# Two graph-attention layers on one core: the last pair's second layer by batch, bias products in three pieces, new orders at both ends, and products of zeros first

## The reference

```python
# layer 0
q, k, v = x @ Wq + bq, x @ Wk + bk, x @ Wv + bv          # per head
attn = softmax(where(adj == 0, -inf, q @ k.T / sqrt(32)))
y = (attn @ v) @ Wo + bo + x
x = layernorm(y) * gamma + beta
# layer 1
q, k, v = x @ Wq.T + bq, x @ Wk.T + bk, x @ Wv.T + bv
pros = softmax(where(adj == 0, -16384, q @ k.T))
z = v
for _ in range(4):
    z = 0.9 * (pros @ z) + 0.1 * v                       # four hops
x = layernorm(x + z) * gamma + beta
```

## Time and profile before

| | us |
|---|---|
| median of three runs | 779.46 |
| runs | 778.97, 779.46, 779.46 |
| the profiled execution | 781.37 |
| its span, first to last instruction | 778.4 |
| TensorE busy in it | 751.4 |
| VectorE busy | 638.4 |
| ScalarE busy | 665.6 |
| GpSimd busy | 548.7 |

### The profile page before, as it was taken

The page is one execution under the profiler, slowest core; times in us unless marked ns, Lnnn a source line. Parts: engine busy times, 40 slices in busy tenths (PEclk is TensorE's granted clock), DMA queues, the critical chain, the costliest instruction groups (busy, mean ns, idle before and its releaser), DMA issues.

```text
span 778.4 us, 32533 instructions
## 1 busy us (share of the span) xinstructions
PE 751.4 (97%) x11544; PEld 708.3 (91%) x11544; DVE 638.4 (82%) x3093; ACT 665.6 (86%) x2570; POOL 548.7 (70%) x417
## 2 busy tenths in 40 slices
PE   6899999999999999999999999999999999999993
PEld 6788999999999999999999999999999999998973
DVE  5878888888888888888888888888888888888866
ACT  4879998889889888989988988998898998899771
POOL 0436858666777877777777777787777787768884
PEclk9999999999999999999999999999999999999998
DMA  7101011010111100111110111111011111000002
GB/s 240 49 21 51 23 35 37 21 31 23 51 49 51 50 27 26 51 51 49 51 39 27 35 51 50 49 51 30 22 51 50 50 50 37 21 11 30 30 15 68
DMA packets 33245, 34.12 MB, mean 44 GB/s; under 512 B 2368, under 2 KB 28864, under 8 KB 33088
## 3 DMA queue, kind: packets, MB, share of 16 engines
q1 hardware_dynamic: 33088, 32.06, 13.6%
HBM read 23.67 MB, written 8.39 MB: 41 GB/s over the span
## 4 chain that ended last, share of the span: by engine, by line
PE 89%; DVE 3%; ACT 2%; issue 1%; POOLq 0%; POOL 0%; DVEq 0%; ACTq 0%
PE psF L344 23%; PE psF L413 18%; PE psF L353 16%; PE psF L403 15%; PE psS L393 9%; PE psF L458 7%; PE psF L438 2%; ACT ex L1013 2%; DVE sm L1402 1%; DVE bst L1452 0%; DVE w_lo L1345 0%; ACT hT L1047 0%; DVE z L1515 0%; DVE hT L1418 0%; ACT pT L1024 0%
## 5 line engine op out<-in xcount | busy, mean ns | idle before, releaser
L1013 ACT ACTIVATE ex<-sm,nmax 128x128 f32<-128x128 f32 x1024 | 398.1, 397 | 3.3 <-DVE nmax L1402 2.3
L1862 POOL TENSOR_TENSOR pr<-ex,rec 128x1024 f32<-128x1024 f32 x128 | 245.4, 1919 | 99.2 <-DVE rec L1411 99.2
L1402 DVE CUSTOM_DVE_ANT_0 sm<-psS,mask 128x128 f32<-128x128 f32 x1024 | 228.3, 284 | 42.4 <-PE psS L393 42.2
L1013 ACT ACTIVATION_READ_ACCUMULATOR ex<-sm,nmax 128x1 f32 x1024 | 200.9, 196 | 0.0
L1024 ACT ACTIVATE pT<-psF 128x512 f32<-128x512 f32 x256 | 138.9, 597 | 34.4 <-PE psF L403 34.3
L403 PE MATMUL psF<-ident,pr 128*128 128x128 f32 x1024 | 137.8, 276 | 0.8 <-ACT pT L1024 0.5
L403 PEld LDWEIGHTS psF<-ident,pr 128*128 128x128 f32 x1024 | 112.7, 141 | 9.3 <-ACT pT L1024 0.9
L344 PE MATMUL psF<-xh,w_hi 128*128 128x256 f32 x512 | 112.2, 301 | 7.8 <-DVE w_lo L1341 5.8
L344 PE MATMUL psF<-xh,w_lo 128*128 128x256 f32 x512 | 103.9, 285 | 0.0
L344 PE MATMUL psF<-xl,w_hi 128*128 128x256 f32 x512 | 103.4, 284 | 0.0
L413 PE MATMUL psF<-pT,z 128*32 128x128 f32 x3072 | 101.5, 274 | 1.8 <-DVE z L1515 1.8
(11 more groups left out here) (76 smaller groups left out, 1426.2 us busy)
## 6 DMA issues: line engine op xcount, KB each, us to landing
xt_in<-in_x_t SPq DMA_DIRECT2D x32, 256.0 KB, 3.1
x_in<-in_x SPq DMA_DIRECT2D x32, 256.0 KB, 2.9
out<-o_t SPq DMA_DIRECT2D x30, 256.0 KB, 2.2
adj_in<-in_adj SPq DMA_DIRECT2D x32, 128.0 KB, 2.4
pT<-in_w SPq DMA_DIRECT2D x4, 256.0 KB, 4.4
row<-in_rows SPq DMA_DIRECT2D x1, 768.0 KB, 7.1
w_raw<-in_w SPq DMA_DIRECT2D x3, 256.0 KB, 7.6
out<-o_t SPq DMA_DIRECT2D x4, 128.0 KB, 1.8
```

What stands on the lines that cost most here:

```text
L1013: e = nc.scalar.activation(ex[l][:, b, h, :], sm[l][:, b, h, :], ACT.Exp, scale=-1.0, bias=nmax[l][:, b, h:h + 1], accum_out=tot[l][:, b, ...
L1402: last = nc.vector.tensor_tensor_reduce(sm[l][:, b, h, :], psS[:, o:o + N], mask[p.parity][:, b, :], -1.0, BIG, ALU.add, ALU.min, nmax[l][ ...
L1862: nc.gpsimd.tensor_tensor(pr[l][:, b, :, :], ex[l][:, b, :, :], rec[l][:, b, :].unsqueeze(2).broadcast_to([128, H, N]), ALU.mult).then_inc ...
```

## The change

1. **Zeros first.** VectorE sets a tile of 256 columns to zero as its first instruction; TensorE waits for it and multiplies it by itself five times, ahead of everything else.
2. **The folds in three pieces.** `folds()` becomes `fold_row` for weight 3 behind the scores of pair 0, `fold_row` for weight 6 between the two keys of pair 1, and `fold_columns` behind them. The saves on VectorE, the rounding and splitting of weights 3 to 6 are dealt out singly.
3. **Orders.** `begin()` now covers t up to 7, the loop runs from 8 to 29, and `end()` covers what was steps 30 and 31 too. In `begin()` and `end()` the order of each engine is dealt anew; `step(t)` is as before.
4. **The last pair's second layer by batch.** For pair 31, layer 1: reciprocals and probabilities for four heads at a time, (0, 0) and (1, 0) on GpSimd, (0, 1) and (1, 1) on VectorE; hops, copies, transposes and adds for one graph at a time, in the banks of the scores, which are free by then; all four copies of a graph on ScalarE; norm and output for one graph at a time.
5. `statistics` waits for the aggregate of the pair before.

```diff
+            nc.vector.memset(zeros[:, :], 0.0).then_inc(zeros_s, 1)
...
+            def keep_warm(times):
+                for _ in range(times):
+                    nc.tensor.matmul(ps_fold[:, :256], zeros[:, :128], zeros[:, :256], start=True, stop=True)
+            pe.wait_ge(zeros_s, 1)
+            keep_warm(WARM)                      # WARM = 5
...
             def begin():                         # TensorE
...
                 free((q_s[0], Pair(0)))
+                values(0, 1, Pair(0))
                 values(0, 0, Pair(0))
-                values(0, 1, Pair(0))
                 scores(0, Pair(0))
-                folds()
+                fold_row(0, 3, ps_fold_bo)
                 free((v_s[0], Pair(0)))
+                queries(0, 1, Pair(1))
                 queries(0, 0, Pair(1))
-                queries(0, 1, Pair(1))
                 free((k_s[0], Pair(0)))
                 keys(0, 0, Pair(1))
+                fold_row(1, 6, ps_fold)
                 keys(0, 1, Pair(1))
+                fold_columns()
...
             def begin():                         # VectorE
+                save_q(0, Pair(0))
                 make_mask(Pair(0))
-                save_q(0, Pair(0))
+                make_mask(Pair(1))
                 save_k(0, Pair(0))
+                split_lo(Pair(1))
                 mask_scores(0, 0, 1, Pair(0))
                 mask_scores(0, 1, 0, Pair(0))
-                split_lo(Pair(1))
                 mask_scores(0, 0, 0, Pair(0))
                 mask_scores(0, 1, 1, Pair(0))
+                save_q(0, Pair(1))
                 save_fold(0)
+                save_k(0, Pair(1))
+                reciprocals(0, 0, Pair(0))
+                split_w(3)
                 save_fold(1)
                 save_fold(2)
-                reciprocals(0, 0, Pair(0))
-                save_q(0, Pair(1))
-                save_k(0, Pair(1))
                 reciprocals(0, 1, Pair(0))
-                split_w(3)
-                make_mask(Pair(1))
...
             def begin():                         # ScalarE
+                round_w(3)
+                split_hi(Pair(1))
                 save_v(0, Pair(0))
-                split_hi(Pair(1))
...
-                for i in range(3, NW):
-                    round_w(i)
+                round_w(4)
                 split_hi(Pair(2))
...
                 save_oh(Pair(0))
+                round_w(5)
+                save_v(0, Pair(1))
...
                 save_x1h(Pair(0))
+                round_w(6)
                 split_hi(Pair(3))
...
             def begin():                         # GpSimd
-                add_bias(Pair(0))
                 probabilities(0, 0, Pair(0))
                 probabilities(0, 1, Pair(0))
+                add_bias(Pair(0))
...
+            def last_hop(j, b):
...
+                src = z[R.parity] if j else v1[R.parity]
+                for c in range(C):
+                    for g in range(G):
+                        h, o = G * c + g, 1024 * b + c * N
+                        last = nc.tensor.matmul(psS[32 * g:32 * g + 32, o:o + N], src[:, b, h * HD:(h + 1) * HD],
+                                                pT1[R.parity][:, b, h, :], start=True, stop=True)
+                last.then_inc(hop_r[b], 1)
+            def last_turn(j, b):
+                pe.wait_ge(hopT_s[b], j + 1)
+                for c in range(C):
+                    o = 1024 * b + 512 + c * 128
+                    last = nc.tensor.transpose(psS[:, o:o + 128], hT[R.parity][:, b * C + c, :], ident[:, :])
+                last.then_inc(turn_r[b], 1)
...
             def end():                           # TensorE, its last lines
                 turn_hop(3, Pair(29))
+                last_hop(0, 0)
+                last_hop(0, 1)
+                last_turn(0, 0)
+                last_turn(0, 1)
+                turn_hop(2, Pair(30))
+                last_hop(1, 0)
+                last_hop(1, 1)
+                hop(3, Pair(30))
+                last_turn(1, 0)
+                last_turn(1, 1)
+                turn_hop(3, Pair(30))
+                last_hop(2, 0)
+                last_hop(2, 1)
+                last_turn(2, 1)
+                last_turn(2, 0)
+                last_hop(3, 0)
+                last_hop(3, 1)
+                last_turn(3, 0)
+                last_turn(3, 1)
...
+            def last_evict(j, b):                # ScalarE
+                act.wait_ge(hop_r[b], j + 1)
...
+                nc.scalar.activation(hT[R.parity][:, b * C:(b + 1) * C, :],
+                                     psS[:, 1024 * b:1024 * b + D].rearrange("p (c n) -> p c n", n=N),
+                                     ACT.Copy, scale=1.0 - ALPHA).then_inc(hopT_s[b], 1)
...
             def end():                           # VectorE, its last lines
                 normalise(1, 0, Pair(28))
                 normalise(1, 1, Pair(28))
                 add_hop(3, Pair(29))
                 statistics(1, Pair(29))
+                last_add(0, 0)
                 aggregate(1, Pair(29))
+                last_add(0, 1)
                 add_hop(2, Pair(30))
                 add_eps(1, Pair(29))
                 normalise(1, 1, Pair(29))
                 normalise(1, 0, Pair(29))
+                last_add(1, 0)
+                last_add(1, 1)
+                add_hop(3, Pair(30))
                 statistics(1, Pair(30))
                 aggregate(1, Pair(30))
                 add_eps(1, Pair(30))
+                last_add(2, 1)
+                last_add(2, 0)
+                finish(1, Pair(30))
                 finish(0, Pair(30))
+                last_add(3, 0)
+                last_add(3, 1)
+                last_statistics(0)
+                last_statistics(1)
+                last_aggregate(0)
+                last_aggregate(1)
+                last_eps(0)
+                last_scale(0)
+                last_eps(1)
+                last_scale(1)
+                last_shift(0)
+                last_shift(1)
...
             def end():                           # GpSimd, its last lines
+                last_probabilities(0, 0)
+                scale_out(Pair(27))
+                restart_term(Pair(31))
+                last_probabilities(1, 0)
+                shift_out(Pair(27))
+                inverse_root(1, Pair(28))
                 scale_residual(Pair(31))
+                inverse_root(1, Pair(29))
+                scale_out(Pair(28))
                 shift_residual(Pair(31))
+                shift_out(Pair(28))
+                inverse_root(1, Pair(30))
                 last_term(Pair(31))
                 scale_out(Pair(29))
                 shift_out(Pair(29))
+                last_root(0)
+                last_root(1)
...
             def statistics(l, p):
+                    dve.wait_ge(ag_s[l].sem, ag_s[l].at(p - 1))
```

More of the change, by code:

```diff
@@ new lines, in end @@
+                mask_scores(1, 0, 0, Pair(27))
+                reciprocals(1, 1, Pair(26))
+                make_mask(Pair(29), last=(0, 0))
+                split_lo(Pair(30))
+                save_ol(Pair(28))
+                mask_scores(0, 0, 1, Pair(29))
+                add_hop(1, Pair(25))
+                normalise(1, 0, Pair(22))
+                save_y(Pair(28))
+                statistics(0, Pair(28))
+                aggregate(0, Pair(28))
+                add_eps(0, Pair(28))
+                save_q(0, Pair(30))
```

1265 lines of the change are left out of this document (862 added, 403 removed).

## The result

| | before | after |
|---|---|---|
| median of five runs, us | 779.42 | **786.31** (786.05 to 786.36) |
| span of the profiled execution | 778.4 | 784.5 |
| VectorE busy in it | 638.4 | 656.9 |

The ratio is 1.0086, with a 95% interval from 1.0075 to 1.0098. Forecast were 775.0 us and at most 777.7: wrong by 11.3 us and in the sign. Two executions are left out of all readings as slow, the profiled one of `e5_open_unlocked` (1063.53 us) and one of `e1_open` (4170.72 us).

The account below looks back on a forecast made before the run. It took TensorE, busy 97% of the span, as the bound, so only opening and drain could change: opening -4.2, last five steps -0.6, pair 31 by batch +0.3, together -4.5 from 779.46 to 775.0 us; range 770.9 to 777.7.

Parts of the forecast that it names:

- The opening: Start of the kernel until TensorE is full: earlier chain and fast clock win 4.2 us, bounds -5.5 and -2.0.
- Zeros done before 5.6: Opening, sign of being right: TensorE's five products of zeros finish before 5.6 us, inside its 5.76 us wait.
- Pairs at 0.24 soon after 6.5: Opening, sign of being right: matmul pairs reach the fast pace, 0.24 to 0.26 us each, soon after 6.5 us.
- First masking near 12.9: Opening: masking of the first scores starts at 12.9 us instead of 13.97, 1.1 us won.
- Layer 1's first scores near 39.0: Opening: layer 1's first scores come at about 39.0 us instead of 43.19; layer 1's queries gain at most 4.0.
- I take the difference to the median: Final sum: the -4.5 us, made on the profiled execution (781.37), is subtracted from the median, 779.46, giving 775.0.
- First failed step: Opening to end: each microsecond won by the opening chain reaches the end whole, as TensorE then only works off a queue.
- The last five steps: Newly ordered steps before the drain: same work, other neighbours; -0.6 us, ends 2.7 gain and about 1 loss.
- Rival 3: Last five steps: newly dealt queues starve TensorE, two waits a step; +7.7 us, time 787, chance 0.04.
- The drain: Pair 31 by batch: shorter rounds, up to 4.4 us, eaten by GpSimd holding VectorE; +0.3, ends -3.8 and +2.5.
- rival 1: Drain: the lock does not bite, last_add(3, 0) within 3.2 us of add_eps(30); drain -3.5, time 771.2, chance 0.25.
- rival 2: Opening clock: zeros don't count as work or one-column products bring slow spell again; opening -2.0, time 777.2, chance 0.17.

Follow-up runs that it names:

- e5_open_unlocked: New opening with old steps and end, single lines moved so GpSimd again waits behind VectorE's normalisations of pairs 1 to 4; 778.47 us, ratio 0.9983.
- e1_open: The changed kernel's opening with the old steps and old drain of the kernel before; 779.67 us, ratio 0.9998.
- e7: Kernel before with only the second layer of the last pair done by batch, all else old; 778.49 us, ratio 0.9982.
- e12: New opening with normalisations released and the first residual shift moved, old steps, last pair by batch; 777.27 us, ratio 0.9962.
- e14: The 777.27 us kernel (new opening released, old steps, last pair by batch) without the products of zeros; 778.62 us, ratio 0.9983.
- e2: Old opening with the changed kernel's last five steps and last pair by batch; 788.06 us, ratio 1.0107.
- e3: Kernel before with the memset and five products of zeros ahead of everything, and the added statistics wait; 780.85 us, ratio 1.0011.
- e9: Old opening, last pair by batch; in the last five steps TensorE and ScalarE in new order, VectorE and GpSimd in old; 786.22 us, ratio 1.0072.
- e4: Kernel before with one loop line moved: VectorE's reciprocals(1, 0) ahead of the two normalise(0, .) instead of behind; 796.73 us, ratio 1.0223.
- e10: Old opening, last pair by batch; only ScalarE in the new order in the last five steps; 786.85 us, ratio 1.0079.
- e11: Old opening, last pair by batch; only TensorE in the new order in the last five steps; 792.21 us, ratio 1.015.

## Why the prediction was wrong

**The opening was right as far as it was followed.** Zeros done before 5.6: 5.15. Pairs at 0.24 soon after 6.5: from 6.04 on. First masking near 12.9: 12.52. Probabilities at 18.4 and 20.8: 17.97 and 20.69. scores(0, 1) near 20.9: 21.14. First save_y 28.9: 28.96. Layer 1's first scores near 39.0: 39.7. TensorE's timeline of after, against the earlier trace rows:

```profile
1.17 3.98 PE L530 MATMUL psF<-zeros 128*128 128x256 f32 x10 [1.17 <-DVE zeros L1943]
...
6.04 0.40 PE L364 MATMUL psF<-xh,w_lo 128*128 128x256 f32 x2
...
11.07 1.17 PE L413 MATMUL psS<-kT,qT 32*128 32x128 f32 x32
...
21.14 1.17 PE L413 MATMUL psS<-kT,qT 32*128 32x128 f32 x32
```

The steps were followed to 43 us, and the -4.2 was -3.5 there. About 1.2 of the 3.5 is the spell of lower clock in before's profiled execution, which other executions of the same opening don't have: against e7 the lead is 2.3. The prediction booked the end of that spell as a gain and then took the whole -4.5 from the median, 779.46, and not from the profiled 781.37. This is a failed step too, if a smaller one: "I take the difference to the median".

**First failed step: "a microsecond by which the opening chain comes earlier reaches the end whole, because behind it TensorE only works off a queue".** `begin()` reaches to 150 us, and its orders were new all the way. TensorE works off a queue only while the other engines deliver; three waits for xn, 1.42, 0.83 and 0.81 us, took back most of the lead. This failed although the prediction had the mechanism in hand: it used the hold of VectorE by GpSimd for `o_t` in the drain and for a mask in the opening, and never asked it of `normalise(0, .)`, around which the diff deals reciprocals and GpSimd's operations anew. Released, the same opening is 1.9 us earlier at the 57th block (e12 against e1).

The Trainium skill, SBUF — State Buffer, on the engine and DMA sides of the memory, says that VectorE and GpSimd share a port pair as an exclusive lock for a whole instruction. These runs agree: two normalisations beside an operation of 1.96 us take 2.26 and not 0.73.

**Second: "The last five steps. Other neighbours, the same work ... I take -0.6 in all", with an end of about +1.** It measured +6.6, more than six times that end. Held normalisations account for 2.2 of it; for the rest the runs leave open whether the order of TensorE and ScalarE or other held operations of VectorE made it. The bound was taken from one wait of the kernel before. Old rows say nothing of a queue that is dealt anew on four engines; they show what the old order achieves. Rival 3 had TensorE starved in these steps and gave 787; 786.31 was measured. Its chance of 0.04 was the error. That its number came so close is partly luck: it added +9.4, +2.5 and -4.2, and the parts measured +6.6, +0.2 and -0.7. The argument against it, that 300 to 400 us has no idle time and so the other queues have slack, took a result of careful ordering for a reserve: the slack of xn is 1.1 us, and a hold is 1.5.

**The drain, term by term.** +0.3 was forecast, +0.2 measured from the 64th block on. Its parts are less close than the sum: pair 31's first hop came 0.5 us later behind the 64th block (16.8 us for 16.3) where 0.6 earlier was forecast, and from this hop to the end it is 20.3 us for 20.6. The held rows came as forecast: in VectorE's timeline of after, `finish(30)` has three operations over 1 us, and the first last_add(3, .) (the row of 778.64) comes 5.4 us after add_eps(30) (773.27), forecast 5.1; rival 1 (under 3.2) is out.

```profile
773.27 0.17 DVE L1825 TENSOR_SCALAR ve<-mv 128x2 f32<-128x2 f32 x1
...
774.53 1.38 DVE L1851 SCALAR_TENSOR_TENSOR o_t<-o_t,rstd,row 128x256 f32<-128x256 f32 x1
775.84 1.48 DVE L1846 SCALAR_TENSOR_TENSOR o_t<-y,mv,row 128x256 f32<-128x256 f32 x1
777.35 1.36 DVE L1851 SCALAR_TENSOR_TENSOR o_t<-o_t,rstd,row 128x256 f32<-128x256 f32 x1
778.64 0.74 DVE L1900 TENSOR_TENSOR y<-psS,zf 128x256 f32<-128x256 f32 x2
```

The price of the hold, 3.8 us between rival 1's -3.5 and the +0.3, is not what the runs show. In e7 `finish(30)` is nearly free (0.89, 0.48, 0.48 and 0.48 us from 767.70 on), and its end is only 0.8 us shorter than after's. TensorE waits 2.00 us there for `z` (ahead of 764.17), behind a VectorE that waits 3.14 us for GpSimd's root.

**The clock (rival 2) did not return.** The granted clock is 1.00 from 16 to 24 us in all nine profiles with the new opening, e14 without zeros among them. The zeros do count as work: without them (e14) the first nine groups of two run at 0.43 us, with them at 0.24. Of the 1.7 us (9 x 0.19) 0.5 to 1.3 are left at the end.

## What to carry to other kernels

Ask of every pair of moved operations on VectorE and GpSimd whether both touch only SBUF (normalisations, conversions and the splits of x and the weights were held here, statistics and reciprocals were not), and what now keeps them apart: an idle moment of GpSimd behind a short operation may be the cheapest interlock of the kernel, and one line in a loop that removed it cost 16 us here. Where a diff deals queues anew, price each part at the end at which its waits could come out, not by the waits of the old order, and test it alone: opening, last steps and drain went -0.7, +6.6 and +0.2; mended, the first is 1.9 us better than it was, the last gives 0.5, and the middle one is left out. Read a lead against several executions of before: here 1.2 us of the opening's lead was a spell of low clock in the one that was profiled. A lead from the opening counts at the last newly ordered step, not where the first full stretch begins.

## What the runs showed of the hardware

- In the collisions of these traces the operation that starts second pays, and since GpSimd's are the long ones, this is mostly VectorE: two of its normalisations grow from 0.73 to 2.26 us, against back-to-back operations to 2.65. GpSimd pays when VectorE was first: `pr` takes 2.23 us for 1.90 where it starts at 23.64, inside VectorE's `w_lo` (23.48 to 24.12) in before, and `xb` 1.73 for 1.31 at 22.55, inside `xl` (21.17 to 23.14) in after.
- Held are not only fp32 normalisations: the conversion of the mask from int32 (1.41 for 0.28 us), `xl` out of `xt_in` (up to 2.38 for 0.68) and the tiny `ve` (up to 1.11 for 0.16) are as well.
- Not everything that touches only SBUF is held. In before, the 84 statistics that started beside a running GpSimd operation took 0.41 us each, as when they ran alone, and 25 reciprocals 0.20 for 0.19. The prediction's "an operation of VectorE that reads only SBUF waits" is too wide by these two. VectorE's masked minima, which read PSUM, kept their 0.28 us.
- The spell of lower clock near 20 us differs between executions of the same opening: among eight profiles with it, the clock from 16 to 24 us was 0.79 twice (before, e2), 0.60 twice (e3, e9) and 1.00 four times (e4, e7, e10, e11), zeros or not. In nine profiles with the new opening it was 1.00.
